# Graph attention on one core: part of VectorE's comparisons joined with the edge mask, GpSimd paced by VectorE's quads, and the end of a group in single pieces

## The reference

```python
Wh = (h @ W.T).reshape(n, K, OUT_DIM).transpose(1, 0, 2)        # n 8192, K 4, OUT_DIM 32
score_src = einsum('knd,kd->kn', Wh, a1)[:, :, None]
score_dst = einsum('knd,kd->kn', Wh, a2)[:, None, :]
e = leaky_relu(score_src + score_dst, 0.2)
e = where((adj == 0)[None], -inf, e)                            # adj 8192 x 8192, int32
alpha = softmax(e, axis=-1)
h_prime = einsum('kij,kjd->kid', alpha, Wh)
x = layernorm(x + h_prime.transpose(1, 0, 2).reshape(n, 128))   # eps 1e-5
```

## Time and profile before

| | before |
|---|---|
| median of 3 runs | 1811.24 us (1807.12 to 1821.82) |
| profiled execution | 1814.96 us |
| its span, first to last instruction | 1813.1 us |
| mean granted TensorE clock | 0.937 of full |
| busy: VectorE | 1676.0 us, 92% |
| busy: ScalarE | 1549.4 us, 85% |
| busy: TensorE | 1483.9 us, 82% |
| busy: GpSimd | 1469.7 us, 81% |
| HBM traffic | 298 MB, 164 GB/s over the span |

### The profile page before, as it was taken

One profiled execution on the slowest core, in us unless ns is written; L12 is line 12 of the kernel. 1 busy time (PEld: TensorE's weight loads), 2 busy tenths in 40 slices (PEclk: granted clock), 3 DMA queues, 4 the chain that ended last, 5 costly groups with the idle time before them and its releaser, 6 DMA issues.

```text
span 1813.1 us, 79728 instructions
## 1 busy us (share of the span) xinstructions
PE 1483.9 (82%) x35235; PEld 1438.9 (79%) x35235; DVE 1676.0 (92%) x1600; ACT 1549.4 (85%) x2567; POOL 1469.7 (81%) x1582
## 2 busy tenths in 40 slices
PE   6207988799898888988888897989888888888886
PEld 4107988799888888888888887988888888888886
DVE  3698989989999999999999999999999999999997
ACT  3369988898989988989888898988988898888974
POOL 0139988989888888989887898888888898878884
PEclk9758999999999999999999999999999999999998
DMA  2406655745656574655556574555656565655540
GB/s 78 135 0 211 194 167 166 208 154 182 183 179 192 168 207 160 201 173 178 187 176 170 166 217 153 193 166 190 175 169 198 161 196 171 192 165 175 167 141 20
DMA packets 161761, 303.04 MB, mean 167 GB/s; under 512 B 9680, under 2 KB 22096, under 8 KB 161424
## 3 DMA queue, kind: packets, MB, share of 16 engines
q1 hardware_dynamic: 161424, 298.03, 52.9%
HBM read 293.67 MB, written 4.33 MB: 164 GB/s over the span
## 4 chain that ended last, share of the span: by engine, by line
issue 26%; ACT 22%; DVE 22%; PE 18%; POOL 4%; DVEq 1%; ACTq 0%; POOLq 0%
ACT step L395 21%; PE bank L666 16%; DVE step L516 8%; DVE step L504 6%; DVE rest L524 3%; POOL edge L301 2%; PE bank L653 2%; POOL step L321 1%; POOL rstd L305 1%; DVE xr L574 1%; DVE late L555 1%; DVE late L558 1%; DVE stats L578 1%; ACT xr L385 1%; DVE late L548 0%
## 5 line engine op out<-in xcount | busy, mean ns | idle before, releaser
L395 ACT ACTIVATE step<-s_all,sd 128x512 uint8<-128x512 f32 x2304 | 1424.5, 716 | 164.0 <-PE bank L666 163.9
L321 POOL TENSOR_SCALAR step<-s_all,sd 128x512 uint8<-128x512 f32 x1280 | 941.4, 755 | 0.0
L666 PE MATMUL bank<-G,step 128*128 128x99 bf16 x16384 | 804.9, 210 | 57.5 <-issue 48.9
L666 PEld LDWEIGHTS bank<-G,step 128*128 128x128 fp8e4 x16384 | 766.9, 99 | 64.5 <-issue 53.4
L301 POOL TENSOR_SCALAR edge<-adj_t 128x2048 int8<-128x2048 int32 x256 | 494.6, 1932 | 204.2 <-DVE step L504 137.8
L516 DVE SCALAR_TENSOR_TENSOR step<-bank,step 128x2048 int32<-128x2048 int32 x256 | 582.5, 2275 | 24.9 <-PE bank L653 20.1
L666 PE MATMUL bank<-F,rest 128*128 128x66 f16 x16384 | 573.7, 197 | 29.4 <-issue 29.2
L524 DVE SCALAR_TENSOR_TENSOR rest<-step,bank 128x2048 int32<-128x2048 int32 x256 | 582.2, 2274 | 6.1 <-PE bank L666 5.6
L666 PEld LDWEIGHTS bank<-F,rest 128*128 128x128 fp8e4 x16384 | 553.0, 100 | 31.8 <-issue 31.6
L504 DVE TENSOR_SCALAR step<-s_all,sd 128x512 uint8<-128x512 f32 x512 | 344.8, 715 | 3.1 <-ACT G L364 3.1
L653 PE MATMUL bank<-identb,edge 128*128 128x128 bf16 x2048 | 163.3, 224 | 185.5 <-DVE rest L524 101.9
(11 more groups left out here) (77 smaller groups left out, 409.2 us busy)
## 6 DMA issues: line engine op xcount, KB each, us to landing
adj_t<-in_adj SPq DMA_DIRECT2D x512, 512.0 KB, 4.9
s_all<-sT_scratch SPq DMA_DIRECT2D x16, 1024.0 KB, 10.1
xr<-in_x SPq DMA_DIRECT2D x32, 256.0 KB, 3.1
out<-xr SPq DMA_DIRECT2D x16, 256.0 KB, 5.7
sT_scratch<-step SPq DMA_DIRECT2D x16, 8.0 KB
a_blk<-in_L_gnn_a SPq DMA_DIRECT2D x8, 0.1 KB, 1.6
step<-in_L_gnn_W SPq DMA_DIRECT2D x1, 64.0 KB, 1.9
```

Of the source, the lines that this page charges most:

```text
L321: last = nc.gpsimd.tensor_scalar(step_u8[:, k % NS, h, n // E, :, n % E], s_all[:, g % 2, h], STEEP, d_steep[:, q * IB + n, h:h + 1], ALU. ...
L395: last = nc.scalar.activation(step_u8[:, q % NS, h, b // E, :, b % E], s_all[:, n, h], ACT.Sigmoid, scale=STEEP, bias=d_steep[:, q * IB + ...
L666: last = nc.tensor.matmul(acc[k][:, col:col + width], matrix[:, h, n // E, b * P:(b + 1) * P, n % E], values[:, q * IB + n, h].rearrange(" ...
```

## The change

Six things change together.

1. The two comparisons of VectorE are done inside `take_step`, for the quad at hand, and as one operation with the edge bytes: `(s_all is_ge d_neg) logical_and edge byte`. The edge byte comes from PSUM through a new byte view `edgeT8`. `compare` is gone, and so is the semaphore `dve_compared`.
2. The and of the words is split: heads 0 to 2 (1536 words) and the half u = 0 of head 3 (256 words). The half u = 1 of head 3 is already masked.
3. GpSimd waits before its comparisons of quad k for `quad_past` >= k - 1. VectorE increments that at the end of each quad, so GpSimd may start quad k once VectorE's list has passed quad k - 2. The wait of `take_edges` for VectorE is gone.
4. `finish` has fewer, slightly regrouped pieces, and `group` takes one a quad, after `take_rest`, from quad 1 on.
5. `take_sums` comes after ScalarE's quad 1 instead of 2, the normalisation after quad 14 instead of 12.
6. The inverse deviation comes after GpSimd's quad 11 instead of 9; SyncE stores rows at quad 4 instead of 2.

```diff
+        edgeT8 = [t[:, :].bitcast(i8).rearrange("p (u i e) -> p u i e", u=U, e=E) for t in tr]
...
-        SCALED = 12
+        SCALED = 14
...
-                    if q == 2 and g > 0:
+                    if q == 4 and g > 0:
...
                 for q in range(QUADS):
                     k = quad_no(g, q)
+                    if k > 1:
+                        pool.wait_ge(quad_past, k - 1)
...
                     if k + N8 < GROUPS * QUADS:
-                        if DVE_TILES:
-                            pool.wait_ge(dve_compared, k + 1)
                         take_edges(k + N8)
-                    if q == 9 and g > 0:
+                    if q == 11 and g > 0:
                         inverse_deviation(g - 1)
...
-                    if q == 2 and not first:
+                    if q == 1 and not first:
                         take_sums(g - 1)
...
-            def compare(g, q, n, waits=True):
...
+            def take_step(g, q, n):
                 nth = at(dve, quad_no(g, q) + 1)
+                if q == 0:
+                    dve.wait_ge(s_loaded[n], 8 * (g + 2 - n))
                 dve.wait_ge(transposed, nth)
+                for b, h in DVE_TILES:
+                    nc.vector.scalar_tensor_tensor(step_u8[:, q % NS, h, b // E, :, b % E], s_all[:, n, h],
+                                                   d_neg[:, q * IB + b, h:h + 1], edgeT8[q % 2][:, b // E, :, b % E],
+                                                   ALU.is_ge, ALU.logical_and)
                 dve.wait_ge(act_compared, nth)
+                dve.wait_ge(pool_compared, nth)
+                nc.vector.scalar_tensor_tensor(step[:, q % NS, 0:HEADS - 1], edgeT[q % 2][:, 0:HEADS - 1], ONES,
+                                               step[:, q % NS, 0:HEADS - 1], ALU.bitwise_and, ALU.bitwise_and)
+                nc.vector.scalar_tensor_tensor(step[:, q % NS, HEADS - 1, 0:WORDS // U], edgeT[q % 2][:, HEADS - 1, 0:WORDS // U],
+                                               ONES, step[:, q % NS, HEADS - 1, 0:WORDS // U], ALU.bitwise_and, ALU.bitwise_and
+                                               ).then_inc(step_set, 1)
...
-                    take_step(g, q)
-                    if q + 1 < QUADS:
-                        compare(g, q + 1, n, waits=not first or q + 1 >= NS)
-                    elif not last:
-                        compare(g + 1, 0, 1 - n)
-                    if q > 1:
-                        next(closing, None)
-                    take_rest(g, q, waits=not first or q >= NL)
-                    if q > 1:
-                        next(closing, None)
+                    take_step(g, q, n)
+                    take_rest(g, q, waits=not first or q >= NL)
+                    if q > 0:
+                        next(closing, None)
+                    dve.sem_inc(quad_past, 1)
```

More of the change, by code:

```diff
@@ L162, in gat_layernorm @@
         act_compared = sem("act_compared")
-        dve_compared = sem("dve_compared")
+        quad_past = sem("quad_past")
         pool_compared = sem("pool_compared")
@@ L494, in _ @@
             dve.wait_ge(f_set, JB // TJ)
-            def compare(g, q, n, waits=True):
-                if DVE_TILES:
-                    if q == 0:
-                        dve.wait_ge(s_loaded[n], 8 * (g + 2 - n))
-                    if waits:
-                        dve.wait_ge(rest_done, at(dve, quad_no(g, q) - NS + 1))
-                    for b, h in DVE_TILES:
-                        last = nc.vector.tensor_scalar(step_u8[:, q % NS, h, b // E, :, b % E], s_all[:, n, h],
-                                                       d_neg[:, q * IB + b, h:h + 1], None, ALU.is_ge)
-                    last.then_inc(dve_compared, 1)
-            def take_step(g, q):
+            def take_step(g, q, n):
                 nth = at(dve, quad_no(g, q) + 1)
+                if q == 0:
+                    dve.wait_ge(s_loaded[n], 8 * (g + 2 - n))
                 dve.wait_ge(transposed, nth)
+                for b, h in DVE_TILES:
+                    nc.vector.scalar_tensor_tensor(step_u8[:, q % NS, h, b // E, :, b % E], s_all[:, n, h],
+                                                   d_neg[:, q * IB + b, h:h + 1], edgeT8[q % 2][:, b // E, :, b % E],
+                                                   ALU.is_ge, ALU.logical_and)
                 dve.wait_ge(act_compared, nth)
-                if POOL_TILES:
-                    dve.wait_ge(pool_compared, nth)
-                if DVE_TILES:
-                    dve.wait_ge(dve_compared, nth)
-                nc.vector.scalar_tensor_tensor(step[:, q % NS], edgeT[q % 2], ONES, step[:, q % NS],
-                                               ALU.bitwise_and, ALU.bitwise_and).then_inc(step_set, 1)
+                dve.wait_ge(pool_compared, nth)
[4 more added lines that the diff above has]
+                                               ).then_inc(step_set, 1)
             def take_rest(g, q, waits=True):
@@ L550, in finish @@
                 wait_last()
+                nc.vector.tensor_tensor(low, low, per_row(beta[:, rows, :], HC), ALU.mult)
                 then(nc.vector.tensor_tensor(top, top, acc_sb[:, :, 2 * HC:BC], ALU.add))
@@ L553, in finish @@
                 wait_last()
-                nc.vector.tensor_tensor(low, low, per_row(beta[:, rows, :], HC), ALU.mult)
                 then(nc.vector.tensor_tensor(top, top, per_row(alpha[:, rows, :], HC), ALU.mult))
@@ L583, in finish @@
                     last = nc.vector.bn_aggr(mv[:, b], stats[:, b])
-                then(last)
-                yield
+                last.then_inc(dve_chain, 1)
+                got[0] += 1
                 wait_last()
-                assert got[0] == CHAIN_STEP
                 nc.vector.tensor_scalar(mv[:, :, 1], mv[:, :, 1], EPS, None, ALU.add).then_inc(var_set, 1)
@@ L590, in finish @@
                     yield
+                assert got[0] == CHAIN_STEP
                 dve.wait_ge(rstd_set, g + 1)
```

2 lines of the change are left out of this document (removed).

## The result

The changed kernel takes 1746.56 us (median of 4, 1744.82 to 1753.74) against 1816.24 us for the kernel before on the same chip (1807.12 to 1821.82). The ratio is 0.963, 95% interval 0.957 to 0.968, so 3.7% faster; forecast were 0.961 and 1741 us. The span of the profiled execution is 1743.0 us, where the sum had 1742.5; that of the second measurement is 1748.8, so single spans of one kernel can differ by some 6 us.

A forecast was written before the change was run, and what follows sets the result against it. VectorE was taken to bound plain quads at 5.80 us. Lead-in, 255 quads at 5.61, 15 group ends at 9.1, leftovers and tail gave a 1742.5 us span, ratio 0.961, so 1741 us; range 1705 to 1790.

The forecast's parts named there:

- the sum: Whole span: 145.9 to the first and, plain quads 1430.6, group ends 136.5, leftovers 7.5, tail 22.0: 1742.5 us.
- The bound: Plain quads: VectorE sets the pace at 5.80 us; the other engines have 0.2 to 0.5 us to spare.
- The joined operation: VectorE's 512-element operation with a PSUM input: 0.743 us long, no queueing with GpSimd, two cost 1.30 us.
- Rival (a): VectorE's joined operation still queues with GpSimd because it reads `s_all` and `d_neg` in SBUF: +159 us, 1900; chance 0.07.
- The plain quad: VectorE's quad without a piece: 1.30 + 1.665 + 0.46 + 2.19 = 5.61 us, 0.19 less than 5.80.
- The wait for the inverse deviation: VectorE's 3.0 us wait before `shift` at each of 15 group ends goes: 45 us.
- The pieces: `finish` on VectorE: double pieces 2.0 us each, single 0.8, small ones about 1.9; 9.1 us a group, bounds 6.8 to 12.1.
- the leftovers: VectorE's waits for transposes that remain at group edges: 0.5 us a group, 7.5 us in all.
- The pace of GpSimd: GpSimd's new wait for `quad_past`: costs nothing, with 0.3 us left in a plain quad.
- The edge of a group: ScalarE's earlier copies free the banks in time; VectorE's transposes waits fall from 1.3 to 0.5 us a group.
- crowded price: VectorE's comparison pair in the kernel before: 1.41 us in plain quads with GpSimd comparing, 0.79 with GpSimd still.

The follow-up runs named there:

- second measurement: The changed kernel again, unaltered, measured later beside other kernels: 1749.89 us, ratio 0.964 to the kernel before.
- 10th run: Changed kernel with the first of the next quad's two joined operations between the and and `rest`, only in quads 4 to 15: 1734.25 us, ratio 0.955.
- ninth run: Changed kernel with the first of the next quad's two joined operations between the and and `rest`, in every quad: 1742.51 us, ratio 0.959.
- fifth run: Changed kernel with the joined operation reading bytes of table G in SBUF instead of edge bytes in PSUM: 1900.61 us, ratio 1.046.
- first run: Kernel before with only VectorE's last piece (`shift`) two quads later, normalisation after quad 14, store at quad 4: 1773.7 us, ratio 0.977.
- sixth run: Changed kernel without `quad_past`, so GpSimd runs as far ahead as the buffers allow: 1760.64 us, ratio 0.969.
- seventh run: Changed kernel with ScalarE's copies of the sums after its quad 2 again instead of 1: 1764.58 us, ratio 0.971.
- fourth run: Changed kernel with separate one-input comparisons and the 2048-word and as before, and without `quad_past`: 1812.34 us, ratio 0.997.
- third run: Changed kernel with separate one-input comparisons and the 2048-word and as before, `quad_past` kept: 1811.03 us, ratio 0.997.
- eleventh run: Changed kernel, one joined operation early in quads 4 to 6 and 10 to 15, piece before `rest` in 1 to 3 and 7 to 9: 1788.95 us, ratio 0.985.
- second run: Kernel before with only the joined operation and split and; old pieces and quad numbers, no `quad_past`: 1785.07 us, ratio 0.983.

## Why the prediction was right

**The bound.** VectorE was the bound in plain quads: taking 0.13 us off them (10th run) moved the time, once the group's edge was left alone. ScalarE had a little more room than the prediction gave it, 5.52 us a quad and not 5.55 (ninth run).

**The joined operation.** Predicted 0.743 us long, the same at every place, and 1.30 for two; measured 743 ns (702 to 753) and 1.32. The reason, that an input in PSUM keeps it clear of GpSimd, is shown by the fifth run: with the input in SBUF 1069 ns and 161 us more. Rival (a) was wrong in the place of its input alone; that its total of 1900 was met as well is in part luck, since the parts were not as it priced them (fifth run).

**The plain quad.** 5.61 predicted, 5.64 measured: the split and 1.67 and 0.44 to `rest` (1.665 and 0.46). But 5.80 was not what the kernel before takes in every plain quad, as the sum assumed: in its first group it ran at 5.64 too, with separate comparisons that fell differently against GpSimd's (1.25 us a pair, at 193.58 in its timeline).

**The wait for the inverse deviation.** 45 us predicted; the wait fell by 45.1, and alone it brought 44.6 (first run, with what balances there).

**The pieces.** 9.1 us a group and 0.5 left over; measured 9.1 in all: from 146.67, the first and, to 1721.40, the last, are 1574.7 us, less 255 x 5.64, by 15. Inside it, errors cancelled. Where no wait for transposes fell into its quad, a double piece cost 1.2 to 1.35 us and not 2.0, since its second operation never waited; the statistics and the other small ones, with the waits in their chain, cost some 2.6 and not 1.9; and every second group loses about 1 us in its last quad, which I had not foreseen. The trace shows where: VectorE's list is a hardware loop over two groups, and behind each of its six branches back the next instruction of the list is recorded 2.8 to 3.1 us later (0.1 where the loop ends), so that VectorE stands idle for 0.9 to 1.3 us once `rest` is done. The kernel before lost as much in the same quads. Why the branch takes this long stays open.

**The total.** It fits better than its terms. The plain quads came to 7.6 us more than in the sum (0.03 each), the ends of the groups with the leftovers to 7.5 less (136.5 against 144.0). That the span came within 0.5 us of the sum is luck, and finer than the 6 us between two executions of this kernel.

**The pace of GpSimd.** Costed at nothing, and it does cost nothing, but it earns 9 to 15 us (sixth run). The sum had it inside the pieces without saying so: the 0.2 us for a single piece assume that GpSimd is at its short comparisons, which is what the pace brings about.

**The edge of a group.** 12 us predicted, 13 to 16 measured, of which only 5.8 are the wait that the prediction named (seventh run).

**The parts do not add as the sum put them.** The joined operation alone brought 30 us, and the later last piece alone 44.6; together 75, and the whole change brought 70. So far it agrees. But all without the joined operation brought 3 us, so the joined operation in the new surroundings is worth 67. What makes separate comparisons so dear there is open (fourth run). The prediction took the comparisons' crowded price as given, 1.41 a pair in plain quads; averaged over all quads a pair keeps VectorE busy for 1.35 us in the kernel before (344.8 / 256) and for 1.53 in the third run (391.1 / 256). The forecast was not hurt, because that price disappears in the changed kernel.

## What to carry to other kernels

When two engines hold each other up at a shared resource, price an operation by where its inputs lie and by what the other engine runs at that moment, not by its rate alone: a slower form that stays clear (743 ns here) can beat a faster one (about 470 alone, 805 in company). Put the small operations of a side chain where the other engine is at its short instructions, and check each place; one four-element operation in the wrong place cost 2.8 us a group. Before filling a gap in a steady stretch, look at the edge of the group too: the same edit gave nothing that can be told when it made the edge need its input earlier, and 0.9% when it kept away from it.

## What the runs showed of the hardware

- A 4-element operation with two inputs in SBUF took 2.99 us, held through the rest of one GpSimd instruction and the whole of the next two, which followed without a gap (eleventh run). I had expected one to be the most.
- Who waits is not settled by length. In a double piece GpSimd's comparison took 1.0 us longer and both additions ran at 0.70; in the kernel before, the second addition (mean 1194 ns) was held in ten of its sixteen executions, to 1.11 us beside a comparison in seven of them and to 2.39 beside the edge bytes in three. Why GpSimd came in between there and not here stays open.
- A 16-element operation with one input in SBUF took 1310 ns on average beside GpSimd (175 to 1900) and 158 in the kernel before (second run), so operations this small are subject to it as well.
- A semaphore increment that stands alone in VectorE's list does not wait for the operations in front of it to end: in the changed kernel `quad_past` counted 0.01 to 0.32 us after the start of the last operation recorded before it, in 211 of 256 cases the 2.29 us `rest`.
